# Gated cross-attention and feed-forward on one core: fewer transfers of q, k, sums and rows, and the score masks of two batches written by TensorE

## What is computed

```
scores = q.k / sqrt(16);  -inf where the mask of (q, k) or the padding of k says so
w = softmax(scores);  att = w @ v;  x = x + tanh(g_xattn) * (att @ Wo.T + bo)
h = layernorm(x)
gate = silu((h @ fp8(gate_w)) * gate_scale);  up = (h @ fp8(up_w)) * up_scale
x = x + tanh(g_ffn) * ((gate * up) @ fp8(down_w)) * down_scale
```

## Time and profile before

| | us |
|---|---|
| median of three runs | 612.08 (609.9 to 614.79) |
| span of the profiled execution, first to last instruction | 616.1 |
| TensorE busy, matmuls | 563.3 (91%) |
| DVE busy | 485.9 (79%) |
| ACT busy | 363.7 (59%) |
| POOL busy | 255.8 (42%) |

### The profile page before, as it was taken

How to read it: one execution, slowest core, us unless ns; L and a number is a source line. 1 busy time by engine, 2 the same in 40 slices (tenths; PEclk the granted TensorE clock), 3 DMA queues, 4 the chain that set the end, 5 groups by cost and what they waited for, 6 DMA issues and landing times.

```text
span 616.1 us, 14167 instructions
## 1 busy us (share of the span) xinstructions
PE 563.3 (91%) x5056; PEld 348.4 (57%) x5056; DVE 485.9 (79%) x1505; ACT 363.7 (59%) x668; POOL 255.8 (42%) x339
## 2 busy tenths in 40 slices
PE   0846888799999999999999999999998999799997
PEld 0633343357754775467745765476645764376683
DVE  2377768999899889988999999988998898744321
ACT  3533675787754765556665576576644764475261
POOL 4043041123552078424464166306711464248274
PEclk9956999699999999999999999999997999799999
DMA  8662465571222033211322412112203000101000
GB/s 299 221 210 85 106 200 113 121 267 37 80 60 73 14 83 111 58 50 40 102 83 70 112 37 81 44 31 66 73 3 95 2 28 29 53 3 53 1 36 34
DMA packets 57158, 50.30 MB, mean 82 GB/s; under 512 B 8000, under 2 KB 46976, under 8 KB 57088
## 3 DMA queue, kind: packets, MB, share of 16 engines
q1 hardware_dynamic: 55600, 48.79, 26.9%
q10 hardware_dynamic: 1488, 0.61, 0.4%
HBM read 35.21 MB, written 9.44 MB: 72 GB/s over the span
## 4 chain that ended last, share of the span: by engine, by line
PE 73%; DVE 13%; issue 8%; POOL 2%; ACT 2%; DMA 1%; POOLq 0%; SPq 0%; DVEq 0%
PE work L982 25%; PE work L993 12%; PE av L890 8%; PE work L921 7%; PE work L960 5%; DVE junk L741 5%; PE sc L862 5%; PE sc L880 4%; DVE ws L750 2%; PE work L931 2%; DMA cin<-in_ctx_t 1%; PE work L907 1%; PE work L941 1%; PE sc L876 1%; PE work L969 1%
## 5 line engine op out<-in xcount | busy, mean ns | idle before, releaser
L741 DVE CUSTOM_DVE_ANT_0 junk<-sc,mq 128x256 bf16<-128x256 f32 x496 | 180.0, 418 | 26.5 <-PE sc L862 26.0
L750 DVE SCALAR_TENSOR_TENSOR ws<-sc,padc,mask_k 128x1024 f32<-128x1024 f32 x112 | 143.3, 1279 | 19.4 <-PE sc L880 18.0
L614 ACT ACTIVATE ws<-ws 128x1024 f32<-128x1024 f32 x112 | 116.8, 1053 | 19.7 <-DVE ws L750 19.4
L538 POOL TENSOR_TENSOR ff<-ga,up 128x256 f32<-128x256 f32 x96 | 69.3, 729 | 120.7 <-DVE ga L826 117.0
L982 PE MATMUL work<-h_h,wg 128*128 128x256 f16 x384 | 90.4, 276 | 0.0
L982 PE MATMUL work<-h_l,wg 128*128 128x256 f16 x384 | 89.8, 274 | 0.0
L982 PE MATMUL work<-h_h,wu 128*128 128x256 f16 x384 | 89.4, 273 | 0.0
L982 PE MATMUL work<-h_l,wu 128*128 128x256 f16 x384 | 89.3, 273 | 0.0
L674 ACT ACTIVATE up<-work,fuse_s 128x256 f32<-128x256 f32 x96 | 45.2, 471 | 55.5 <-PE work L982 55.5
L993 PE MATMUL work<-wd,f_h 128*128 128x512 fp8e4 x192 | 73.0, 380 | 0.1
L993 PE MATMUL work<-wd,f_l 128*128 128x512 fp8e4 x192 | 72.8, 379 | 0.0
(11 more groups left out here) (116 smaller groups left out, 1013.6 us busy)
## 6 DMA issues: line engine op xcount, KB each, us to landing
qs<-q_scratch SPq DMA_DIRECT2D x96, 64.0 KB, 2.4
xin<-in_x SPq DMA_DIRECT2D x8, 512.0 KB, 4.6
cin<-in_ctx_t SPq DMA_DIRECT2D x8, 512.0 KB, 4.5
xb<-in_x SPq DMA_DIRECT2D x8, 512.0 KB, 4.7
att_u<-un SPq DMA_DIRECT2D x128, 32.0 KB, 2.0
out_x<-yt SPq DMA_DIRECT2D x16, 256.0 KB, 2.2
ks<-k_scratch SPq DMA_DIRECT2D x48, 64.0 KB, 2.4
q_scratch<-qh SPq DMA_DIRECT2D x16, 128.0 KB, 2.5
```

Of the source, the lines that this page charges most:

```text
L538: pool.tensor_tensor(ff[:, n % RING, :], ga[:, n % RING, :], up[:, n % RING, :], ALU.mult).then_inc(ff_done, 1)
L614: act.activation(ws[:, unit, :, :], ws[:, unit, :, :], ACT.Exp, scale=1.0 / SSC).then_inc(exp_done, 1)
L741: last = dve.tensor_tensor_reduce((junk, junk_1)[maxima_banks(n, b)][:, j, :], sc[maxima_banks(n, b)][:, place(j)], mq[b % 2][:, t, :], 1. ...
L750: dve.scalar_tensor_tensor(out=ws[:, n % 4, :, :], in0=sc[1][:, :].rearrange("p (j l) -> p j l", j=HPG), scalar=padc[b % 2][:, kt:kt + 1], ...
```

## The change

1. `BY_PE` is 2: batch 1's 16 scores get their mask by two matmuls each, and DVE leaves out 16 of its 112 instructions of line 750.
2. q's and k's scratch tensors have the order of the tiles that read them (the columns of Wq, Wk and the rows of Wo are permuted on the way in so that one strided transfer writes a half). Writing takes three transfers (the half that is used twice is written twice), in two pieces for the high and the low half; reading takes two instead of six, each of 48 partitions with 4 KB in one piece.
3. `rows` takes two transfers instead of four, `den` one instead of four, `gather` four instead of eight. Both pieces of `spread` now need both pieces of `gather`.
4. The set-up pieces have names and a semaphore each; the context's first transfer moves to ACT's queue behind Wk's; Wo, the masks and the small loads move into SP's list.
5. All five lists of order are written anew. TensorE begins with `xT*2 k q*2 xT*2 v maxima*2 q maxima*7 mrow q scores` where it began with `k xT*2 q*2 v xT*2 maxima*3 q maxima*6 mrow q maxima k maxima scores`.

```
-BY_PE = 1
+BY_PE = 2
...
+        def q_part(n, part):
+
+            return q_dram[n][:, HD * part:HD * (part + 1)].rearrange("f d p l -> (d p) f l")
+
+        def k_part(part):
+            return k_dram[HD * part:HD * (part + 1)].rearrange("d g l -> (d g) l")
...
+                if name == "put_qh":
+                    sp.wait_ge(q_high, 2 * b + n + 1)
+                    past(sp, qs_in[n], 32 * b)
+                    for part in (0, 2):
+                        sp.dma_start(q_part(n, part), qh[:, 2 * n:2 * n + 2, :]).then_inc(q_out[n], 16)
+                if name == "put_ql":
                     wait_free(sp, "q", n, b)
...
+                    past(sp, qs_in[n], 32 * b)
+                    sp.dma_start(q_part(n, 1), ql[:, 2 * n:2 * n + 2, :]).then_inc(q_out[n], 16)
                 if name == "get_q":
-                    sp.wait_ge(q_out[n], 32 * (b + 1))
+                    sp.wait_ge(q_out[n], 48 * (b + 1))
                     past(sp, t_ready, 16 * (b - 1))
                     for hf in range(2):
-                        for s in range(3):
-                            src = q_dram[(0, 1, 0)[s], 2 * n * P:2 * (n + 1) * P, :]
-                            sp.dma_start(qs[b % 2][64 * hf + HD * s:64 * hf + HD * (s + 1), 8 * n:8 * n + 8, :],
-                                         src.rearrange("(p f d) n -> f d p n", f=2, d=HD)[hf]).then_inc(qs_in[n], 16)
...
+                        sp.dma_start(qs[b % 2][64 * hf:64 * hf + 3 * HD, 8 * n:8 * n + 8, :],
+                                     q_dram[n, hf]).then_inc(qs_in[n], 16)
...
                     for v, rows in ((0, nm_h), (1, nm_l)):
-                        for hf in range(2):
-                            row = 64 * hf + 3 * HD + v
-                            sp.dma_start(qs[b % 2][row:row + 1, 8 * n:8 * n + 8, :],
-                                         rows[8 * hf:8 * hf + 8, :]).then_inc(mr_in, 16)
+                        sp.dma_start(qs[b % 2][3 * HD + v:P:64, 8 * n:8 * n + 8, :], rows[:, :]).then_inc(mr_in, 16)
...
-                    for j in range(HPG):
-                        sp.dma_start(den[G * j:G * j + G, :],
-                                     un[32 * j + HD:32 * j + HD + 1, :, :]).then_inc(den_in, 16)
+                    sp.dma_start(den[:, :], un[HD:P:32, :, :]).then_inc(den_in, 16)
...
-                    for gp in range(2):
-                        for j in range(HPG):
-                            at = 64 * gp + HD * j
-                            sp.dma_start(att_u[at:at + HD, 2 * n:2 * n + 2, :],
-                                         un[32 * j:32 * j + HD, 4 * n + gp:4 * n + 4:2, :]).then_inc(att_in[n], 16)
+                    for j in range(HPG):
+                        at = 64 * n + HD * j
+                        sp.dma_start(att_u[at:at + HD, :, :],
+                                     un[32 * j:32 * j + HD, 4 * n:4 * n + 4, :]).then_inc(att_in[n], 16)
```

More of the change, by code:

```diff
@@ new lines @@
+    xT*2 k q*2 xT*2 v maxima*2 q maxima*7 mrow q scores maxima k scores maxima xT*2 scores maxima weighted
+    scores maxima scores maxima v maxima scores maxima weighted scores maxima mrow q scores maxima weighted
+    scores maxima scores maxima weighted scores maxima weighted scores maxima k scores maxima weighted scores
+    maxima q mrow maxima scores weighted maxima scores maxima scores weighted maxima scores maxima scores
+    weighted scores maxima spread scores spread weighted maxima xT*2 scores maxima out scores maxima mrow out
@@ new lines @@
+    weighted maxima q scores maxima q scores maxima weighted x2T*2 scores maxima v gu scores maxima weighted gu
+    scores maxima gu scores maxima gu scores maxima weighted gu mrow scores maxima gu scores maxima gu scores
+    maxima weighted gu scores weighted k maxima scores gu weighted scores maxima gu*3 v maxima scores spread
+    down_a maxima scores down_a weighted scores maxima spread mrow down_b scores maxima out xT weighted maxima
+    scores xT out maxima q maxima scores down_b weighted maxima scores x2T*2 q maxima scores gu*2 weighted
@@ new lines @@
+    weighted maxima scores gu scores gu v down_a scores maxima weighted spread scores down_b maxima scores
+    spread down_a xT scores maxima weighted down_b xT maxima out maxima scores mrow out q weighted scores maxima
+    q x2T*2 maxima scores weighted k gu maxima scores gu maxima weighted scores gu maxima scores gu scores gu
+    maxima mrow gu maxima scores weighted gu scores maxima gu weighted maxima scores v weighted maxima scores gu
+    maxima gu scores maxima gu weighted scores down_a scores gu weighted spread maxima scores down_a spread
@@ new lines @@
+    maxima scores down_b mrow maxima scores out*2 maxima scores weighted xT*2 down_b maxima scores weighted k
+    x2T maxima scores q scores maxima x2T q weighted scores maxima gu*2 maxima scores weighted gu scores maxima
+    gu maxima mrow gu scores maxima gu weighted maxima scores gu weighted scores maxima gu*2 maxima scores gu*2
+    weighted maxima scores gu down_a spread maxima scores down_a weighted scores spread maxima down_b mrow
+    scores maxima out scores weighted scores out weighted scores down_b scores weighted maxima scores x2T*2 v
@@ new lines @@
+    scores gu maxima gu maxima scores gu maxima gu weighted maxima scores gu maxima gu maxima scores mrow gu
+    maxima gu maxima weighted scores gu maxima scores weighted gu scores maxima gu scores weighted gu down_a
+    scores maxima spread weighted scores down_a spread maxima down_b maxima scores out mrow scores out weighted
+    scores down_b scores weighted x2T scores x2T weighted scores gu scores gu scores gu weighted scores gu
+    weighted scores gu*2 weighted gu*4 spread gu spread gu out*2 down_a*2 x2T down_b x2T down_b gu*12 down_a*2
@@ L181 @@
+    get_q put_qh load_xb put_kl rows gather put_ql store get_q put_ql gather store get_k den get_q rows gather
+    load_xb rows den gather store rows store load_xb gather den store gather store*5
 """)
```

326 lines of the change are left out of this document (157 added, 169 removed).

## The result

After the change the kernel takes 594.47 us (median of 4 runs, 593.5 to 596.1) where the runs of the kernel before beside it took 612.54 (4 runs): a ratio of 0.9709 with an interval of 0.9678 to 0.9739, 18 us less. The forecast was 602 with a range of 587 to 613. The profiled execution took 594.84 us with a span of 593.0, against a span of 616.1 before. A time is some 1.8 us longer than its span, so the profiled execution of before lies 5 to 6 us above its median, which matters for the sums further down.

What follows compares the result with a forecast made beforehand. TensorE bounds the kernel from the first gu at 141.5 us, DVE close behind and setting the pace just before. Terms -7.6 - 3.8 - 2.4 + 4.8 = -9.0, 1 us more off for stalls: 612.08 - 10.0 = 602, range 587 to 613.

Steps and rivals of the forecast that it cites:

- rival 3: Whole kernel: new lists shrink all stalls, also behind the first gu; 593 us, 588 at best; chance 0.20 (under 597).
- Term A: Start up to first maxima: earlier normalization, q and reads bring it from 39.29 to 31.7 us; -7.6 (-4 to -11).
- Term B: First maxima to first scores: earlier mrow, shorter row transfers, one k and two maxima moved later; -3.8 (-6 to 0).
- The narrow transfers: Row transfers in term B: spread over 2 engines instead of 8, estimated to cost nothing beyond 2.4 us of landing.
- Term C: First scores to first gu: masks and moved work add, DVE's stall shrinks; -2.4 (bounds +5.2 and -9.6).
- Term D: Behind the first gu: six masked scores and moved pieces add work, stalls unchanged; +4.8 (bounds -8 and +13).
- I leave them as they are: Stalls behind the first gu, some 14.6 us with half the low clock's time, were assumed unchanged.
- Rival 1: Batch 1's scores: TensorE stands while ACT holds the bank, 17.6 us plus 8 of masks; 621 us; chance 0.07 (over 618).
- Rival 4: Fewer transfers, but nothing waited for them and loads bind the start; 610.5 us; chance 0.23 shared with rival 2.
- none of it is on TensorE's path: SP's read and write issues, 24 more and 96 fewer over 8 batches, don't delay TensorE while it is the bound.

Runs made afterwards that it cites:

- e11: Kernel before with half of batch 5's down product and one weighted product moved later in batch 7's order; 617.58 us, ratio 1.010.
- e5: Changed kernel, its lists and layout kept, with reads, rows, sums and gathers in as many transfers as before; 657.69 us, ratio 1.075.
- e8: Changed kernel with DVE's shift1 ahead of columns and ACT's norm1 ahead of its two cT; 595.59 us, ratio 0.974.
- e4: Changed kernel with batch 1's masks back on DVE (BY_PE = 1), filled into its new list; 605.51 us, ratio 0.987.
- e2: Kernel before with the new scratch layout and fewer transfers, old lists, old first loads, BY_PE at 1; 612.03 us, ratio 0.999.
- e1: Kernel before with batch 1's masks on TensorE and two ACT exponentials moved up, old lists and transfers otherwise; 629.09 us, ratio 1.026.
- e3: Kernel before with new layout, fewer transfers and batch 1's masks on TensorE, two ACT exponentials moved earlier, old lists otherwise; 627.25 us, ratio 1.023.
- e7: Changed kernel with DVE's shift1 ahead of columns; 594.81 us, ratio 0.972.

## Why the prediction was right

The time came out 7.5 us under the forecast and inside the range. Of the signs named, the first matmul missed (15.0, not 12 to 13), while the first maxima (31.4), scores (50.0) and gu (125.3) came near their 32, 52 and 128. But 594.5 lies in the band under 597 that rival 3 had, with 0.20, and not in the forecast's own: the terms ahead of the first gu were sized well, and the one behind it was not. By its own terms, each from the two profiled executions:

- **Term A** (forecast -7.6): 31.43 against 39.29, -7.9. The sum is right and its parts are not. TensorE's start came later, 15.01 and not "12 to 13", and the reads landed later than the 2.4 us taken from the earlier trace rows, at a median of 3.6 us for three times the bytes. That median hides more: this read released TensorE at 31.43, 4.7 us behind its second issue. Two things paid for it. One is the clock: the 24 matmuls took 2.92 us where half of 8.31 was counted. (That half, 4.2, mixes both clocks; at the low one the first 24 of before took 5.1, so "half of 8.31 at the low clock" was misread.) The other is the writing of the low half, after which the first read could be issued 2.0 us later and not 3.4.
- **Term B** (-3.8): 18.56 against 23.6, -5.0. `mrow` came 12.2 us behind the first maxima, not 14.5: q's matmuls took 2.7 us at the high clock and hid behind DVE's nine maxima, 12.4 by the prediction's own figure. The rows took 6.3 us, not 5.3: SP's first issue came 3.0 us behind `mrow` and not 2.0, since POOL's low half took 1.64 us where it had taken 0.66.
- **The narrow transfers.** The last row was issued at 47.39 and released TensorE at 49.99, 2.6 us later and 2.1 behind the issue's end. By the rule that was weighed there (the Trainium skill, "DMA: Bandwidth & Descriptors", "Why a DMA increments its semaphore by 16 and not by 1") the transfer goes over fewer engines. Rows cut as before released TensorE 1.2 us behind the end of their last issue (e11 at 523.36, and most places of e5), so the 2.4 taken from q's row was too long for them. Rows in two transfers did so in 1.23 us at the same place in e8, but in 2.1 in after. So the narrow form need cost next to nothing, and up to 0.9 us of cost in after can't be excluded.
- **Term C** (-2.4): 125.50 - 50.0 = 75.5 against 78.6, -3.1. Of the 5.6 us that TensorE stood in the last stretch ahead of the first gu, 2.95 are left, and the clock is 1.00 instead of 0.86. DVE under 90% was named as the sign, and it is 82%. e4 shows that this is the masks' doing on these lists: with them on DVE the stretch takes 86.2 us instead of 75.3, from first scores to first gu.
- **Term D** (+4.8, and 1 us taken off in the sum): 593.0 - 125.5 = 467.5 against 474.6, -7.1. This is the term that was mis-sized, by 11.9 us in these two executions, in "I leave them as they are". The idle time behind the first gu is 7.0 us instead of 12.2 (1.54, 0.83, 0.09 and 4.5 at the very end), which is 5.2. The rest is busy time: TensorE was to be busy 4.8 us more and was busy 1.9 less, 6.7 us, about what the low clock had cost between 461 and 550 (0.16 x 89 / 2 = 7.1). Part of that is one execution's. From 455 to 475 us before and e2, and e11 too, have the same three waits of TensorE, 0.18, 0.35 and 1.84 us, and the same 17.63 us busy, yet the clock is 0.83 in before and 1.00 in the two others. Against e2's execution, 471.3 us from its first gu at 136.6 on, D is -3.8 (5.0 less idle, 1.2 more busy), and the term was mis-sized by 8.6. Either way it is rival 3's mechanism, put at 0.20, with its D of -3 still too small.

The sum of the measured terms, -7.9 - 5.0 - 3.1 - 7.1, is the 23.1 us between the two spans. The medians differ by 18: the profiled execution of before lay above its median, as the prediction said. Some 3 us of the difference is the clock in term D, and some 2 to 3 lie at the start. e11, whose lists and transfers are those of before up to 500 us, has its first maxima at 37.52, first scores at 60.67 and first gu at 138.76, against 39.29, 62.87 and 141.43. So A is between -6.1 and -7.9, and B and C are the same within half a microsecond.

Rival 1 was right in its mechanism, and nearly in its price, but for another kernel: on the old lists (e1, e3). Its 25.6 us (17.6 and 8) less term C's 7.6 of DVE's relief are 18, and e1 lost 17, 14.7 of them in masks that waited for ACT in the whole run where before had 2.0. The argument against it, that TensorE has other pieces between two scores, holds only where the list puts ACT's exponential early enough. Rival 4, fewer transfers for which nothing waited in the end, is e2 on the old lists: 612.0 us where the rival had 610.5. Neither holds for the change as a whole, since the lists were written for it: they count on few issues and on DVE's free time. The prediction costed the lists only by what they move ahead of the first gu, and "none of it is on TensorE's path" of SP's issues is true of the old order; in the new one 27 to 34 us hang on each half of them.

What stays open: which moves of the new lists mend the late stalls. The run that tried one of them (e11) shows that it isn't that one alone. And what the new lists would gain over the old transfers if SP's list were laid out for those was not tried beyond one word; nor was e1 with an ACT list laid out for its masks, or e4 with a DVE list laid out for its own.

## What to carry to other kernels

Where the order of every queue is written out, an edit and the lists are one change: the same edit of the masks was worth +17 us on one set of lists and -11 on another. So ask of each freed resource which list can use it, and of each wait what stands behind it in the same queue. A piece that fills a gap may already cover another: look at the waits on both sides of the place that it leaves before it is moved. And price a stall with the low clock that may follow it: here 5 us of idle time went, and 3.6 to 6.7 us of busy time with it, since the same stall was followed by the low clock in one execution and not in two others.

## What the runs showed of the hardware

- A pause can cost TensorE more than its length. In the kernel after it works from 15.01 on with gaps of at most 0.15 us on the chain, and q's matmuls from 19.66 on take 0.12 us each (2.92 / 24). In e7 it stops at 16.2, when a matmul of k already took 0.11, begins again at 18.28 at 0.11 and goes over to 0.21 at 18.6, so that the mean of the 24 is 0.19 (4.46 / 24).
- It need not: waits of 0.18, 0.35 and 1.84 us at the same place of the work, with the same 17.63 of 20 us busy, left the clock at 1.00 in e2 and in e11 and at 0.83 in before.
- The granted clock reads 1.00 from 15 to 20 us in after, where matmuls of 256 columns start 0.21 us apart, and 0.11 apart from 20.1 on. At the start of a kernel the spacing of matmuls tells the clock and the column doesn't.
- An issue costs SP about as much for 8 KB as for 192: 0.39 to 0.50 us for a read of 192 KB, 0.44 for one of 64 KB, 0.73 for a gather of 32 KB, 0.52 to 0.67 for a row of 8 KB. The landing grows with the size but far less than in proportion: 3.6 us for 192 KB against 2.2 for 64 KB of the same layout (e5) and 2.4 in the kernel before. On these lists 216 more issues in SP's in-order queue, with the same bytes, were worth 63 us.
